# Index copies on GpSimd and a second scatter round in flight, in a four-layer graph network on one core

## The reference

```
h = relu(layernorm(x)); x = x + relu(segment_sum(h[src] @ w_rel[type], dst) + h @ w_loop + b)
h = relu(layernorm(x)); x = x + attention over edges, summed by src (4 heads)
h = relu(layernorm(x)); x = x + sage(relu(ln(sage(h))))      # two SAGE steps
h = relu(layernorm(x)); x = x + gcn(h)
sage(h) = h @ W_self.T + (segment_sum(h[src], dst) / count) @ W_neigh.T + b
gcn(h)  = D^-1/2 (A + I) D^-1/2 h @ W
```

## Time and profile before

| | us |
|---|---|
| median of 3 runs | 3975.69 (3972.27 to 3983.72) |
| the profiled execution, its own time | 3976.37 |
| its span | 3974.6 |
| DVE busy | 2483.4 (62%) |
| PE busy | 2580.5 (65%) |
| POOL busy | 2474.8 (62%) |
| ACT busy | 1729.4 (44%) |

### The profile page before, as it was taken

How to read it: one execution, slowest core, us unless ns; L and a number is a source line. 1 busy time by engine, 2 the same in 40 slices (tenths; PEclk the granted TensorE clock), 3 DMA queues, 4 the chain that set the end, 5 groups by cost and what they waited for, 6 DMA issues and landing times.

```text
span 3974.6 us, 66355 instructions
## 1 busy us (share of the span) xinstructions
PE 2580.5 (65%) x14044; PEld 2047.2 (52%) x14044; DVE 2483.4 (62%) x10828; ACT 1729.4 (44%) x4561; POOL 2474.8 (62%) x2378
## 2 busy tenths in 40 slices
PE   5888868884665655000898676566766774666666
PEld 3444446664555554000786555455655664556666
DVE  6777769894554544787666655444566565556666
ACT  2333337774444443011445555311344444555555
POOL 5777736667888887445776555577544445764443
PEclk9999989997777777555667766655788875569989
DMA  7355538883333332897224666522577773226766
GB/s 270 123 194 213 194 131 271 271 265 72 41 41 41 41 41 34 271 313 238 52 52 132 222 222 214 158 52 52 181 237 237 229 244 90 53 57 216 224 220 216
DMA packets 328229, 638.48 MB, mean 161 GB/s; under 512 B 61072, under 2 KB 89776, under 8 KB 321992
## 3 DMA queue, kind: packets, MB, share of 16 engines
q1 hardware_dynamic: 233406, 501.99, 38.2%
q0 software_dynamic: 90944, 133.85, 14.8%
q10 hardware_dynamic: 3786, 1.65, 0.2%
HBM read 371.35 MB, written 277.50 MB: 163 GB/s over the span
## 4 chain that ended last, share of the span: by engine, by line
DMA 19%; POOL 18%; issue 14%; DVE 5%; ACT 2%; PE 1%; POOLq 0%; DVEq 0%; SPq 0%; ACTq 0%
DMA sums<-parked,last_i 14%; POOL sums L764 11%; POOL got L732 7%; DMA got<-rowsg,gidx 3%; DVE out_stats L1691 2%; DMA got<-rows,gidx 1%; PE bank L1163 1%; DVE out_mv L1698 1%; ACT out_sd L1066 1%; ACT e_h L901 1%; DVE n_t L1791 1%; DVE e_stats L1473 0%; DVE den L1783 0%; DMA rows<-ring 0%; DMA ring<-sums 0%
## 5 line engine op out<-in xcount | busy, mean ns | idle before, releaser
L764 POOL DMA_INDIRECT sums<-parked,last_i x588 | 604.5, 1028 | 670.7 <-DMA sums<-parked,last_i 505.9
L732 POOL DMA_INDIRECT got<-rows,gidx x588 | 603.8, 1027 | 213.7 <-issue 167.9
L1027 ACT ACTIVATE n_h<-ring 128x128 f32<-128x128 f32 x1176 | 483.3, 482 | 211.7 <-DVE ring L1747 131.3
L1306 PE MATMUL bank<-ring,ident 128*128 128x128 f32 x2352 | 508.8, 302 | 0.0
L1303 PE MATMUL bank<-w_t,n_ht 128*128 128x128 f32 x1568 | 360.4, 357 | 135.8 <-DMA ring<-sums 135.7
L1173 PE MATMUL bank<-parked 128*128 128x512 f32 x784 | 374.9, 622 | 78.7 <-DVE parked L1565 76.1
L1279 PE MATMUL bank<-ident,n_h 128*128 128x128 f32 x1176 | 225.7, 323 | 303.4 <-ACT n_h L1027 283.0
L1306 PEld LDWEIGHTS bank<-ring,ident 128*128 128x128 f32 x2352 | 410.4, 218 | 0.0
L1163 PE MATMUL bank<-ident,e_h 128*128 128x128 f32 x588 | 137.8, 378 | 400.1 <-ACT e_h L901 399.5
L1303 PEld LDWEIGHTS bank<-w_t,n_ht 128*128 128x128 f32 x1568 | 290.0, 253 | 200.6 <-DMA ring<-sums 163.3
L778 POOL DMA_INDIRECT attsums<-ring,sidx x196 | 312.3, 1593 | 79.7 <-issue 63.5
(11 more groups left out here) (190 smaller groups left out, 6631.9 us busy)
## 6 DMA issues: line engine op xcount, KB each, us to landing
ring<-sums SPq DMA_DIRECT2D x392, 264.0 KB
ring<-rows SPq DMA_DIRECT2D x392, 264.0 KB, 3.7
rows<-ring SPq DMA_DIRECT2D x294, 264.0 KB, 3.8
ring<-attsums SPq DMA_DIRECT2D x98, 264.0 KB
rowsg<-ring SPq DMA_DIRECT2D x98, 264.0 KB, 3.2
ring<-rowsg SPq DMA_DIRECT2D x98, 264.0 KB, 4.8
sums<-parked SPq DMA_DIRECT2D x16, 1584.0 KB
attsums<-parked SPq DMA_DIRECT2D x16, 1584.0 KB
```

What stands on the lines that cost most here:

```text
L732: pool.indirect_dma_start(out=got[:, b, j, 0:width], out_offset=None, in_=table[:, :], in_offset=bass.IndirectOffsetOnAxis(ap=gidx[:, b, j ...
L764: pool.indirect_dma_start(out=sums[:, :], out_offset=bass.IndirectOffsetOnAxis(ap=last_i[:, t:t + 1], axis=0), in_=parked[:, t, :], in_off ...
L1027: last = nc.scalar.activation(n_h[:, b, k, :], x_data(phase, g)[:, k, :], ACT.Relu, bias=x_col(phase, g, k, COL_C), scale=x_col(phase, g, ...
L1306: last = nc.tensor.matmul(o, lhsT=ident[:, :], rhs=s_rows(phase, g)[:, k, 0:D], start=False, stop=(bias is None or k == K - 1))
```

## The change

Two things change in the chased phases, and only there.

First, the indices of a scatter no longer come from `last_i` directly. A ring of 16 columns, `tidx`, holds them: before each scatter GpSimd copies the column of the next tile, `tidx[:, (t+1) % 16] <- last_i[:, t+1]` (128 x 1, int32), and each scatter waits at `tidx_ready` for the copy of its own tile, which was issued one tile earlier. There are 196 copies in each of 3 phases, and a gate in front of every scatter in place of one a round.

Second, `round_landed(r - 1)` now stands behind `scatter_parked(r)`, so that the 4 scatters of round r are issued before GpSimd waits for those of round r - 1.

```diff
--- before.py
+++ after.py
@@ -239,6 +239,7 @@
 
         gidx = sb("gidx", [P, GOT, TPR], i32)
         didx = sb("didx", [P, 2, TPR], i32)
+        tidx = sb("tidx", [P, 16], i32)
         sidx = sb("sidx", [P, GOT, TPR], i32)
         slot_keys = sb("slot_keys", [P, 2, 3, TPR], bf16)
         got = sb("got", [P, GOT, TPR, W])
@@ -365,6 +366,7 @@
         rounds_landed = Signal(sem("rounds_landed"), 1, 1)
         parked_ready = Signal(sem("parked_ready"), 1)
         scattered = [Signal(sem(f"scattered{b}"), 16 * TPR) for b in range(2)]
+        tidx_ready = Signal(sem("tidx_ready"), 1)
 
         a_h = Signal(sem("a_h"), 2, 8)
         a_turned = Signal(sem("a_turned"), 2, 4)
@@ -756,13 +758,20 @@
                     pool.wait_ge(scattered[b].sem, (parity_first(seg_index(phase), b) + r // 2 + 1) * 16 * TPR)
                     pool.sem_inc(rounds_landed.sem, 1)
 
+                def copy_index(t):
+                    nc.gpsimd.tensor_copy(tidx[:, t % 16:t % 16 + 1], last_i[:, t:t + 1])\
+                        .then_inc(tidx_ready.sem, 1)
+
                 def scatter_parked(r):
                     pool.wait_ge(parked_ready.sem, parked_before(phase) + r + 1)
-                    gate(pool)
                     for j in range(TPR):
                         t = r * TPR + j
+                        if t + 1 < TILES:
+                            copy_index(t + 1)
+                        pool.wait_ge(tidx_ready.sem, CHASED.index(phase) * TILES + t + 1)
+                        gate(pool)
                         pool.indirect_dma_start(
-                            out=sums[:, :], out_offset=bass.IndirectOffsetOnAxis(ap=last_i[:, t:t + 1], axis=0),
+                            out=sums[:, :], out_offset=bass.IndirectOffsetOnAxis(ap=tidx[:, t % 16:t % 16 + 1], axis=0),
                             in_=parked[:, t, :], in_offset=None,
                             bounds_check=bound, oob_is_err=False).then_inc(scattered[r % 2].sem, 16)
 
@@ -801,9 +810,12 @@
                     else:
                         pool.wait_ge(h_ready.sem, h_ready.credit + normalised_before(phase) + ROUNDS)
                     gate(pool)
+                    copy_index(0)
                     for r in range(ROUNDS):
                         scatter_parked(r)
-                        round_landed(r)
+                        if r > 0:
+                            round_landed(r - 1)
+                    round_landed(ROUNDS - 1)
 
                 def fetch_dst(r):
```

## The result

The changed kernel takes 3620.0 us (median of 4 runs, 3617.8 to 3621.9) beside 3976.9 for the kernel before; the ratio is 0.910, 95% interval 0.9085 to 0.9117.

A forecast was written before the change was run, and what follows sets the result against it. The prediction took GpSimd's scatter issue and landings to bound the three chased phases. Rounds falling to 6.75, 8.25 and 6.40 us over 48 rounds gave 218 us less, signals 3 more: 3760 us from 3976.4, range 3685 to 3875.

The forecast's parts named there:

- What bounds the kernel before: Chased phases: GpSimd's scatter issue and its own landings set the pace, 8.10, 9.77 and 8.08 us a round; node work waits.
- the 6% on top of the bounds: All three phases: close bounds do not meet perfectly, so some 6% on the largest: 6.75, 8.25 and 6.4 us a round.
- the 3 us for the signals: Landing signals now stand behind the next round's issue: 1 us a phase, 3 us in all.
- GpSimd's tile: Scatter, 0.19 us copy and 0.30 us gap in the chased phases: 1.54, 1.57 and 1.46 us a tile.
- The copies' hold by DVE: DVE operations with two SBUF inputs delay GpSimd's copies: 0.24 us a round in SAGE0, 0.6 in SAGE1.
- The bound by the DMA engines: Same bytes at ATT's 0.94 busy share: shortest rounds 5.9, 7.7 and 6.0 us in SAGE0, SAGE1 and GCN.
- The chain of ACT and PE: Node phase of SAGE0 and GCN, ACT waiting for PE's transpose: about 3.2 and 3.0 us a group, 6.4 and 6.0 a round.
- D: Rival: the bounds are met without loss, rounds of 6.4, 7.7 and 6.0 us; 281 us less, 3695 us; chance 0.12.
- A: Rival: the node side binds earlier, DMA share 0.85, rounds 7.0, 9.0 and 7.05 us; 139 less, 3840 us; chance 0.22.
- B: Rival: each scatter pays 0.82 us behind its copy, rounds 8.5, 8.9 and 7.9 us; 31 less, 3945 us; chance 0.08.
- C: Rival: each scatter pays 1.32 us, rounds 10.5, 10.9 and 9.9 us; 254 us more, 4230 us; chance 0.04.
- E: Rival: landings stretch by as much as is overlapped, only the copies' cost remains; 115 us more, 4090 us; chance 0.04.

The follow-up runs named there:

- the order alone: Changed kernel without the ring copies: scatters read `last_i` directly and two rounds are under way; 3613.6 us, ratio 0.9086 to the kernel before.
- the kernel with two copies: Changed kernel with one more copy of the same index column for each tile, into another buffer; 3680.8 us, ratio 0.9256 to the kernel before.
- all three edits: Changed kernel without copies, ACT normalising before taking the previous group's transposed rows in SAGE0 and GCN, SP loading due rounds once for two groups; 3610.2 us.

## Why the prediction was wrong

**What bounds the kernel before** held. The loop of issue and landing set the pace of all three phases; with it gone the wait of SP is gone, and the order alone gives the whole gain.

**The size of the miss, term by term.** The forecast took 1.35, 1.52 and 1.68 us a round off the three phases. The stages fell by 109.2, 139.7 and 108.9 us, which over 48 rounds is 2.3, 2.9 and 2.3. Of the 142 us by which the sum fell short, the 6% on top of the bounds is 48 x (0.35 + 0.55 + 0.40) = 62; the bounds themselves were 28 us too high in SAGE0 (6.4 a round), 40 in SAGE1 (7.7, the DMA engines) and 9 in GCN (6.0); the 3 us for the signals are the rest.

**GpSimd's tile** was priced at 1.54, 1.57 and 1.46 us, with the copies' hold at 6.4, 6.9 and 5.9 us a round. From first to last scatter the rounds measure 5.7, 6.3 and 5.4 us, so the tiles 1.43, 1.58 and 1.36 with the hold in them. The gap behind a copy is 0.16 us and not 0.30; the nearest row was the one that I kept as the lower end, 0.17 behind an unrelated instruction. The copies' hold by DVE was about right, and so was the Trainium skill's rule (SBUF — State Buffer, Who interferes with whom) as far as it speaks of the copies: 280, 346 and 194 ns with one, three and no such operation. Its inference that descriptor writing is spared is not borne out: without copies the scatters themselves average 1113 ns in SAGE0 and 970 in GCN, and in SAGE0 1.25 us where they overlap such an operation. What the dearer tile would have cost is 61 us: the kernel with two copies has about the rounds of my working and takes 3681.

**The bound by the DMA engines and the 6% on top** are the steps that failed most: 3760 less 3681 leaves 79 us that a right price of the tile does not explain. The DMA bound set the sum in SAGE1, at 7.7 us a round where GpSimd's was 6.9. I took ATT's share of 0.94 for a ceiling; SAGE1 reached 1.01 and 341 GB/s, 380 GB/s with all three edits, and leaving out a fifth of the bytes changed no stage by more than 5 us. So a share near 1 is not the sign of a bound. That it fills up when more loads are queued is my reading, and no run here measured the engines' own limit. ATT's own 314 GB/s need not have been a ceiling either: DVE is busy for 0.88 of that stretch. For SAGE1 this step left 1.52 us a round to gain, with the 6%, where 2.9 were gained.

**The loss of 6% where bounds meet** was not there. In SAGE0 GpSimd's round, (2405.39 - 2126.30)/48.75 = 5.7 us, and the chain's at full clock, 5.8, lie side by side, and the node phase kept up with the scatters: it ended 28 us after the last one started, where it had been 24 (2543.73 - 2520.02). The kernel with two copies says the same at about the rounds of my working: it takes 1.79 and 2.08 us a round off SAGE0 and GCN, where the bounds without any loss, 6.4 and 6.0, give 1.70 and 2.08. Why nothing is lost, whether by the buffers between the engines, was not tried.

**The chain of ACT and PE** was rightly named; its size was off because I took the clock for given. At a granted clock of 0.71 I put it at 3.2 us a group; with fewer waits PE is granted 0.97 and it is 2.88. A forecast that takes waits away from PE should price its steps at the rows of full clock.

**SP** was not among my bounds, and in SAGE1 it is the first: 3.2 us and more of its queue a group, with 4 us of waits in 290, and 20 us less of the stage when half of its register loads go. The prediction spoke of it only as one that waits.

**The rivals.** D, all bounds met without loss, was the nearest and was still 75 us too long; by the stages it is 40 in SAGE1, from the DMA bound, and 28 in SAGE0 and 9 in GCN, from GpSimd's tile, the clock taken for the chain and, in GCN, the DMA share. A, B, C and E are refuted: the node side is not slower, no gap of 0.8 us stands behind a copy, and landings take next to nothing of GpSimd's time (0.2 us in 208).

What stays open is how much of the changed kernel's time the clock's rise gave. No run held it fixed.

## What to carry to other kernels

When a wait leaves a loop, list the next bound of every queue, SP's included, from rows at full clock and from the closest spacing that each engine shows; a rate seen elsewhere in the kernel is a ceiling only if nothing else held it there. A DMA share near 1 does not say that the transfers are the bound; a run with fewer bytes, or one that moves the same in less time, does. Where two bounds are equal, single edits show nothing, and both have to be lifted at once.

## What the runs showed of the hardware that I had not expected

- A GpSimd copy of 128x1 between two indirect DMAs costs 0.06 us net: 0.19 us of copy, and the gap before the next DMA falls from 0.30 to 0.16.
- DVE's operations with two SBUF inputs hold an indirect DMA's issue too: 1.25 us for the scatters that overlap one, 0.975 for the others, in the same stretch of SAGE0. With a copy ahead of each the scatter is 982 ns and the copy 280: the hold moves, the sum stays.
- Behind a wait for a landing the DMA starts about as soon with a copy ahead of it as alone: 0.94 us after the landing beside 0.90.
- The mean DMA share can read 1.01 and not be the bound: SAGE1's 361 us with that share became 331 with the same transfers.
- With a copy between every two of them, 4 indirect DMAs took 0.2 to 0.5 us longer to issue, and the round with its landing took no longer, within 0.04 us.
